# Two transformer blocks on one core: two fp16 parts for q and k, scores of two heads together, bias tiles and some weight splits on GpSimd

## The reference

```python
xn = layernorm(x)
x = x + attn0(xn) + experts(xn)        # block 0
xn = layernorm(x)
x = x + attn1(xn) + ternary_ffn(xn)    # block 1

# attn0, 16 heads of 16: bias from rel * slope and a causal mask
scores = q @ k.T * 16 ** -0.5 + rel * slope[h]; scores[causal] = -inf
attn = maximum(softmax(scores), 1e-10)
# experts: 8 of 256 -> 256 -> 256, all computed, weighted by token
out = sum_e w[e] * ((silu(xn @ Wg[e]) * (xn @ Wu[e])) @ Wd[e])
# attn1: the same without slopes and without the clamp
# ternary_ffn: W1 (1024x256) and W2 (256x1024) become alpha * sign(W) where |W| > delta
delta = 0.05 * max|W|; alpha = sum(|W| where |W| > delta) / count
y = gelu(xn @ W1q.T + b1) @ W2q.T + b2
# the result y of all 8 batches is rounded to 15 levels of one scale
scale = max|y| / 7 + 1e-8; y = clip(round(y / scale), -7, 7) * scale
```

## Time and profile before

| | |
|---|---|
| median of 3 runs | 858.34 us |
| the profiled execution | 856.29 us |
| its span on the core | 854.6 us |
| mean granted TensorE clock | 0.918 |
| PE, DVE, ACT, POOL busy | 684.0, 614.7, 588.4, 178.2 us |
| first pass | 0 to 142.4 us |
| six steady passes | 142.4 to about 697.5 us |
| last pass, final pass | to about 803 us, to 854.6 us |

### The profile page before, as it was taken

How to read it: one execution, slowest core, us unless ns; L and a number is a source line. 1 busy time by engine, 2 the same in 40 slices (tenths; PEclk the granted TensorE clock), 3 DMA queues, 4 the chain that set the end, 5 groups by cost and what they waited for, 6 DMA issues and landing times.

```text
span 854.6 us, 19350 instructions
## 1 busy us (share of the span) xinstructions
PE 684.0 (80%) x5856; PEld 539.7 (63%) x5856; DVE 614.7 (72%) x2239; ACT 588.4 (69%) x1753; POOL 178.2 (21%) x205
## 2 busy tenths in 40 slices
PE   0686544889878997989798997899798978897756
PEld 0464433668756785868676875688576856685533
DVE  3978746887677876787688767787678776766364
ACT  2455421887759794888488775979498848966764
POOL 6011021132113211131113211321113111320222
PEclk9889876999989998999989997999899999998975
DMA  6752005040413123130504040312313050300661
GB/s 194 267 148 87 1 1 160 2 148 16 128 48 111 37 79 108 40 109 13 174 1 148 13 145 30 111 37 87 100 57 91 13 160 2 124 26 1 191 202 52
DMA packets 55195, 73.94 MB, mean 87 GB/s; under 512 B 4544, under 2 KB 47680, under 8 KB 55104
## 3 DMA queue, kind: packets, MB, share of 16 engines
q1 hardware_dynamic: 52064, 69.22, 26.2%
q0 software_dynamic: 1056, 2.62, 1.0%
q10 hardware_dynamic: 1984, 1.21, 0.5%
HBM read 42.10 MB, written 30.93 MB: 85 GB/s over the span
## 4 chain that ended last, share of the span: by engine, by line
PE 39%; ACT 19%; DVE 18%; issue 15%; DMA 6%; ACTq 1%; SPq 1%; DVEq 1%; POOL 1%; POOLq 0%
PE gen_ps L972 9%; PE gen_ps L983 6%; ACT probs L875 5%; PE value_ps L1056 4%; PE gen_ps L1015 4%; DVE probs L1321 3%; PE gen_ps L946 3%; DVE probs L1332 3%; PE gen_ps L1003 3%; ACT hid L859 3%; ACT pt L884 3%; PE turn_ps L1033 2%; PE gen_ps L958 2%; PE turn_ps L1035 2%; PE turn_ps L1034 2%
## 5 line engine op out<-in xcount | busy, mean ns | idle before, releaser
L875 ACT ACTIVATE probs<-probs,nmax 128x256 f32<-128x256 f32 (+1 forms) x512 | 227.3, 447 | 57.1 <-DVE nmax L1321 55.8
L1321 DVE CUSTOM_DVE_ANT_0 probs<-score_ps,bias 128x256 f32<-128x256 f32 (+1 forms) x512 | 158.6, 352 | 62.8 <-PE score_ps L1027 60.1
L744 POOL TENSOR_TENSOR h_lo<-hid,h_hi 128x512 f16<-128x512 f32 x64 | 76.0, 1187 | 419.6 <-ACT h_hi L852 405.1
L884 ACT ACTIVATE pt<-turn_ps 128x384 f32<-128x384 f32 x256 | 121.4, 477 | 38.5 <-PE turn_ps L1035 38.5
L972 PE MATMUL gen_ps<-xe_hi,gu_hi 128*128 128x256 f16 x512 | 103.8, 287 | 5.2 <-DVE v_sb L1192 4.6
L972 PE MATMUL gen_ps<-xe_lo,gu_hi 128*128 128x256 f16 x512 | 103.7, 286 | 0.0
L972 PE MATMUL gen_ps<-xe_hi,gu_lo 128*128 128x256 f16 x512 | 103.5, 286 | 0.0
L875 ACT ACTIVATION_READ_ACCUMULATOR probs<-probs,nmax 128x1 f32 x512 | 97.4, 190 | 0.0
L1026 PE MATMUL score_ps<-k_stack,q_stack 96*128 96x256 bf16 x256 | 72.9, 287 | 28.8 <-DMA k_stack<-scr_k 15.2
L1033 PE MATMUL turn_ps<-ident,probs 128*128 128x128 f32 x256 | 76.7, 299 | 21.0 <-DVE probs L1332 15.7
L1332 DVE TENSOR_SCALAR probs<-probs,rsum 128x256 f32<-128x256 f32 (+1 forms) x256 | 87.5, 384 | 4.6
(11 more groups left out here) (169 smaller groups left out, 1530.0 us busy)
## 6 DMA issues: line engine op xcount, KB each, us to landing
q_stack<-scr_q SPq DMA_DIRECT2D x32, 384.0 KB, 3.9
k_stack<-scr_k SPq DMA_DIRECT2D x32, 384.0 KB, 5.1
scr_q<-parts SPq DMA_DIRECT2D x16, 384.0 KB, 2.7
scr_k<-parts SPq DMA_DIRECT2D x16, 384.0 KB, 3.3
scr_q<-parts SPq DMA_DIRECT2D x16, 256.0 KB, 3.6
scr_k<-parts SPq DMA_DIRECT2D x16, 256.0 KB, 3.6
x<-in_x SPq DMA_DIRECT2D x8, 256.0 KB, 3.0
scr_q<-parts SPq DMA_DIRECT2D x16, 128.0 KB, 2.9
```

Source lines behind the costliest of these rows:

```text
L744: pool.tensor_tensor(h0_lo[:, e], hid0[:, e], h0_hi[:, e], ALU.subtract).then_inc(s_h0l, 1)
L875: last = act.activation(probs[:, k, lo:hi], probs[:, k, lo:hi], ACT.Exp, scale=-1.0, bias=nmax[:, k, j:j + 1], accum_out=total)
L884: act.activation(pt[:, slot:slot + 3].rearrange("p t q -> p (t q)"), turn_ps[s % 2][:, 0:3 * P], ACT.Copy).then_inc(s_ev, 1)
L1321: last = dve.tensor_tensor_reduce(out=probs[:, k, lo:hi], in0=g[:, lo:hi], in1=bias[:, blo:S], scale=-1.0, scalar=BIG, op0=ALU.add, op1=AL ...
```

## The change

1. **Two fp16 parts.** q and k are cut into two fp16 parts, so 4 products x 16 features, 64 rows. `r0`, `r1`, `m0`, `m1` are gone. `l0`/`l1` subtract once, from `rest` and the first part. A batch stores with four DMAs in place of six; a group of eight heads is loaded with four DMAs of 64 rows and half the heads each.
2. **Paired heads.** Odd heads lie on partitions 64 to 127 of the same operands. PE issues the scores of both heads at the even one, four matmuls, into both score banks, when all maxima before them have been taken.
3. **Bias tiles** are made by GpSimd: a cast and 8 instructions on 128x1024.
4. **Weight splits** 3, 5, 7, 9, 11 and 13: the low part by GpSimd, for which ACT scales the raw tile in place as well (one more copy of 128x1024 each).
5. **Over partitions.** The five all-reduces are replaced: PE turns the column of 128 values (steps `tmx`, `tsm`, `qmax`, each takes a `gen_ps` bank), DVE reduces over the free axis.
6. **Ternary sums.** GpSimd multiplies weight and signs (128x2048), ACT sums that and the squares of the signs with its accumulator, two passes.
7. **Reciprocal** of 128x16 sums, then a copy to 128x256.
8. In the final pass `w2` and `qmax` lose their lag of 8 places on DVE (now 1 and 0). Steps of one name are kept in turn by `in_turn`; `gate` and the first `down` of a pass have one more wait each.

```diff
-SPLITS = 6
+SPLITS = 4
...
-    ln1a rt1 0 ln1b gate:0 1 up:0 tr1 2 3 rt2 gate:1 q1 k1 4 r1 down:0 5 6 v1 up:1 m1 7 gate:2 w1:0 w1:1 w1:2
+    ln1a rt1 0 ln1b gate:0 1 up:0 tr1 2 3 rt2 gate:1 q1 k1 4 down:0 5 6 v1 up:1 7 gate:2 w1:0 w1:1 w1:2
...
+POOL_SPLITS = (3, 5, 7, 9, 11, 13)
...
-                    wait(sp, s_lo, i - 1)
+                    sp.wait_ge(*lo_done(i - 2))
...
+                if name == "setup" and st.arg == 1:
+                    pool.tensor_copy(rel, rel_i).then_inc(s_pool, 1)
...
+                    for c in range(4):
+                        four, shape = slice(4 * c, 4 * c + 4), [P, 4, S]
+                        pool.tensor_tensor(bias0[:, four], rel.unsqueeze(1).broadcast_to(shape),
+                                           slope_sb[:, four].unsqueeze(2).broadcast_to(shape), ALU.mult).then_inc(s_bias, 1)
+                        pool.wait_ge(s_bias, 2 * c + 1)
+                        pool.tensor_tensor(bias0[:, four], bias0[:, four], bias1[:].unsqueeze(1).broadcast_to(shape), ALU.add)\
+                            .then_inc(s_bias, 1)
+                if name == "split" and st.arg in POOL_SPLITS:
...
+                    pool.tensor_tensor(lo, raw[st.arg % 2], hi, ALU.subtract).then_inc(s_lop, 1)
...
-                    pool.partition_all_reduce(t_amax[:, i:i + 1], t_max[:, i:i + 1], P, R_MAX).then_inc(s_tp, 1)
...
+                if name == "tern" and st.arg % TERN_STEPS == 4:
...
+                    act.activation(w, w, ACT.Copy, accum_out=t_sum[:, i, 0:1]).then_inc(s_ts, 1)
...
+                    act.activation(w, t, ACT.Square, accum_out=t_sum[:, i, 1:2]).then_inc(s_ts, 1)
...
+                if name == "tmx":
...
+                    pe.transpose(g[:, 0:P], t_max[:, st.arg:st.arg + 1].broadcast_to([P, P]), ident[:]).then_inc(full[st.bank], 1)
...
-                    wait(pe, s_mx, heads_before(st, -1))
+                    wait(pe, s_mx, heads_before(st))
...
+                    for hp in range(2):
+                        pe.matmul(score_ps[hp][:, 0:S], q[rows[hp], i, P:S], k[rows[hp], i, :], start=True, stop=True)
...
-                if name in ("r0", "r1"):
...
-                                   esum1[:, st.arg % H // 8].rearrange("p t h -> p (t h)").unsqueeze(2)
+                    dve.tensor_copy(rsum1[:].rearrange("p t h c -> p (t h) c"),
```

More of the change, by code:

```diff
@@ L150, in order_of @@
             out.append((name, int(arg or 0), int(word.startswith("+")) - int(name in BLOCK1)))
-    return with_heads(out, last)
+    steps = iter(in_turn([x for x in out if not isinstance(x, int)], lambda x: (x[0], x[2], x[1])))
+    return with_heads([x if isinstance(x, int) else next(steps) for x in out], last)
 SPLIT = [("qk", 0), ("gu", 0), ("wd", 0), ("gu", 1), ("gu", 2), ("wd", 2), ("gu", 3), ("gu", 4), ("wd", 4), ("gu", 5),
          ("gu", 6), ("wd", 6), ("gu", 7), ("qk", 1)]
+POOL_SPLITS = (3, 5, 7, 9, 11, 13)
 def uses(order):
@@ L210, in stages @@
         users = last_users(kind, it)
-    out, place, after_down = [], 0, {}
+    out = []
+    places = {step[0:2]: i for i, step in enumerate(x for x in ORDERS[kind] if x[0] in ("down", "op0"))}
     use = USES_BEFORE[kind]
@@ L220, in stages, with behind @@
         if st.name == "up":
-            st.place = after_down.get(st.arg - 2, 0)
+            st.place = places.get(("down", st.arg - 2), -1) + 1
         if st.name in ("down", "op0"):
-            st.place = place
-            place += 1
-            if st.name == "down":
-                after_down[st.arg] = place
+            st.place = places[st.name, st.arg]
         out.append(st)
-    late = [i + lag.get(f"{st.name}:{st.arg}", lag.get(st.name, 0)) for i, st in enumerate(out)]
-    return [out[i] for i in sorted(range(len(out)), key=lambda i: (late[i], i))]
+    def behind(st):
+        for key in (f"{kind}.{st.name}:{st.arg}", f"{kind}.{st.name}", f"{st.name}:{st.arg}", st.name):
+            if key in lag:
+                return lag[key]
+        return 0
+    late = [i + behind(st) for i, st in enumerate(out)]
+    return in_turn([out[i] for i in sorted(range(len(out)), key=lambda i: (late[i], i))],
+                   lambda st: (st.name, st.n.off, st.arg))
 def last_users(kind, it):
@@ L935, in do @@
                     last.then_inc(full[st.bank], 1)
+                if name == "tmx":
+                    pe.wait_ge(s_t, TERN * st.arg + 1)
+                    g = take(st)
+                    pe.transpose(g[:, 0:P], t_max[:, st.arg:st.arg + 1].broadcast_to([P, P]), ident[:]).then_inc(full[st.bank], 1)
+                if name == "tsm":
+                    pe.wait_ge(s_ts, 2 * st.arg + 2)
+                    g = take(st)
+                    for a in range(2):
+                        last = pe.transpose(g[:, P * a:P * a + P], t_sum[:, st.arg, a:a + 1].broadcast_to([P, P]), ident[:])
+                    last.then_inc(full[st.bank], 1)
+                if name == "qmax":
+                    pe.wait_ge(s_q, 1)
+                    g = take(st)
+                    pe.transpose(g[:, 0:P], yred[:, 0:1].broadcast_to([P, P]), ident[:]).then_inc(full[st.bank], 1)
                 if name in ("q0", "k0", "q1", "k1"):
@@ L1093, in do @@
                        .then_inc(s_set, 1)
[L1094 to L1102 removed]
+                if name == "split" and st.arg not in POOL_SPLITS:
                     i = st.arg
[L1104 removed]
+                    dve.wait_ge(s_hi, his_done(i))
                     hi, lo = split_parts(i)
@@ L1379, in by_channel @@
     def by_channel(w):
-        w = w.reshape(-1, H, C).transpose(0, 2, 1)
+        heads = [8 * u + 2 * i + hp for u in range(2) for hp in range(2) for i in range(4)]
+        w = w.reshape(-1, H, C)[:, heads].transpose(0, 2, 1)
         return w.reshape(-1, P, 2).transpose(0, 2, 1).reshape(-1, H * C)
```

223 lines of the change are left out of this document (120 added, 103 removed), and 2 rows, old and new, of the table LAG.

## The result

The changed kernel takes 875.19 us (median of 4 runs, 871.66 to 876.3) where the kernel before took 858.47. The ratio is 1.0184 with a 95% interval of 1.0151 to 1.0218: it is slower, by 1.5 to 2.2%, where -32 us were forecast. The profiled execution took 871.66 us, with a span of 869.9 against 854.6, so 15.3 us are to be found in the two traces.

A forecast was written before the change was run, and what follows sets the result against it. No engine is full; waits bound it, the first pass set by DVE and what it waits for, a steady pass by PE. 856.3 - 11 - 15.6 - 4 - 1.5 = 824.2, 826 us on the median's basis; range 803 to 850.

The forecast's parts named there:

- Front, +12: Start of first pass: first scores at about 61 us, 12 us later, behind GpSimd's bias instructions and split 5; bounds +1 to +18.
- I put 1 us for each of four, so -12.6: Rest of first pass: DVE's 16.6 us of waits for GpSimd's all-reduces become 1 us for each of four, -12.6.
- if it came early: Rest of first pass: PE would stand behind GpSimd's product and ACT's sums if early, but the order leaves room.
- Half of DVE's 15.3 us in the first pass: Rest of first pass: 15.3 us of splits, sum passes and `r0` leave DVE; half counted, -7.6.
- I take +1.0 there and nothing at the other 15 pairs: Steady pass: waiting for all earlier maxima costs PE +1.0 us at heads 14 and 15, nothing at the other pairs.
- rival C: Slower: score banks no longer alternate, PE waits for the second maximum at 128 pairs, +48 us, 874 us; chance 0.13.
- over 4 us a pass: Sign in the steady passes: PE's idle time released by a maximum under 2 us a pass; over 4 is rival C.
- I take -0.05: Steady pass: scores of a pair on different rows gain 0.05 us, over 16 pairs -0.8 us a pass.
- Steady gaps, -2.6: Steady pass: of 3.25 us in three PE gaps ending with the probabilities' copy or scaling, 2.6 go.
- the terms without the pair: Steady pass: -2.6 us from PE's gaps and -0.2 from freed DVE time behind the last head.
- Last and final pass, -5.5: Last pass -4 us from reciprocal, copies and subtraction on the chain; final pass -1.5 from one reciprocal.
- The bounds of the first pass: Whole first pass: -11 us, from -20 (all DVE work, front +6) to +2 (front +18, stalls alone gained).

The follow-up runs named there:

- e2: Changed kernel, but bias tiles and all low parts of the weight splits made by DVE as in the kernel before; 863.45 us.
- e11: Changed kernel with splits 3 and 5 made by DVE, bias tiles and the other splits staying on GpSimd; 868.16 us.
- e9: Changed kernel with the PE steps tmx and tsm for the ternary weights, and the DVE steps after them, moved 1 to 4 places later in the first pass; 869.53 us.
- e3: Changed kernel, but maxima and sums over partitions of the ternary weights are GpSimd all-reduces again, and the two sum passes DVE's; 881.78 us.
- e7: Kernel before, but PE issues both heads' scores at the even one, once all earlier maxima are taken; 96 rows, no row groups; 888.8 us.
- e4: Changed kernel with the edits of e1, e2 and e3 together; 870.8 us.
- e5: Kernel of e4, but score operands have 96 rows again, 64 of data and 32 of zeros, with one load each for q and k; 839.22 us.
- e1: Changed kernel, but each head's scores are issued at its own place and wait for all maxima but the last one; 876.51 us.
- e6: Changed kernel with the edits of e1, e2 and e5, keeping its maxima and sums by PE, GpSimd and ACT; 835.99 us.

## Why the prediction was wrong, step by step

- **Front, +12: right,** +11.5. The line through the two rows gave 2.35 us for 128x1024; the additions took 2.34 where alone, the products 1.89. That GpSimd's work does it is shown by e2; that the load for split 7 waits ahead of the stores, by e11, where the first scores come 6.7 us earlier without that wait. e11 also shows a second mechanism that was priced too low: DVE itself is held up, 8.8 us there, even in its smallest instructions. I had counted 0.87 us for each of three to five meetings, and on GpSimd's side.
- **"I put 1 us for each of four, so -12.6": failed.** DVE's 16.6 us went, but it waits 9.0 for the turns, and the turns that replace the all-reduces stand in PE's queue and hold up everything behind them, 23.4 us. PE also came back slower: it stood idle for 7.6 us up to 83.91 and for 7.1 up to 114.82, and behind each stall the granted clock is at 0.50, the lower of its two levels (1.2 of 2.4 GHz), for over 5 us of work:

```profile
83.90:89.50 5.60, 5.59 (x32) 2.96 (x33) 2.88 (x11) 3.25 (x7) 1.10 (x1) 0.50 0.02 5
...
114.80:120.00 5.20, 5.18 (x25) 3.77 (x26) 1.59 (x5) 1.44 (x5) 0.00 (x0) 0.50 0.00 0
```

  The prediction has no term for that; PE's busy time behind the first scores rose by 3.7 us. I had written that PE would stand behind the sums "if it came early" and took from the order, without following it in time, that it would not. e9 shows it was the place: moved back by a few steps they cost 7.5 us. By e3 this part is still worth 6.6 us, not 12.6.
- **Half of DVE's 15.3 us in the first pass: mostly lost.** DVE's busy time fell by 7.6 us and not by the 15.3 of the work that left, because the time in which it is held up counts as busy. Beside the GpSimd product of 2048 columns the scaling of one head at 100.46 took 3.83 us instead of 0.55. How much of the rest is held-up time was not added up, and the 7.6 us didn't shorten the part.

```profile
99.87 4.07 POOL L811 TENSOR_TENSOR hid<-hid,t_sb 128x2048 f32<-128x2048 f32 x1 [5.02 <-DVE t_sb L1185]
```

```profile
100.46 3.83 DVE L1392 TENSOR_SCALAR probs<-probs,rsum 128x256 f32<-128x256 f32 x2
...
104.95 0.55 DVE L1392 TENSOR_SCALAR probs<-probs,rsum 128x256 f32<-128x256 f32 x2
```

- **"I take +1.0 there and nothing at the other 15 pairs": failed.** It is +4.8 in a steady pass (5.1 against 0.3), in four waits, and 55.9 - 13.4 = 42.5 us over the program, 0.33 per pair, above the 0.25 from which rival C decides. By the prediction's own sign (over 4 us a pass) that is rival C. e7 shows that the early wait costs 30.5 us by itself. I had looked for the step that DVE was ahead by in the kernel before, where the second score of a pair comes later; issuing it earlier uses up just that lead.
- **"I take -0.05" for a pair: failed.** At the place shown above it is +0.08 (0.42 against 0.34). That the rows run side by side was right, and a price of 0.14 for leaving the mode was read from the earlier trace rows; but going in costs another 0.09 and going out 0.15, in all 0.24. On average over a pass the pair term is nearer 0, since PE is as busy as before, where -0.8 was forecast. In the changed kernel this price only takes away what side by side gains; with single heads, which visit twice as often, it costs 31.6 us (e4 to e5), and that is why taking out the pair alone (e1) did not help.
- **Steady gaps, -2.6: the right kind, too large.** The gaps before value products and turns fell by 25.5 us over the program, but in e5, without the early wait and without 64 rows, only by 5.9 (38.3 to 32.4). Where neither pairs nor rows disturb, in e5, a steady pass is 1.1 us shorter, where the terms without the pair were -2.8.
- **Last and final pass, -5.5: right in sum,** -6.3, though not in place. The last pass gained nothing; that the pair's price took it there too is likely and was not tested by itself. The end gained 6.5, of which 3.9 is one store of x; no run tells whether that belongs to the change.

The chain at that place before, and after with the copy that took the reciprocal's place:

```profile
802.92 6.08 DMA x_dram<-yx_sb
```

```profile
824.73 2.17 DMA x_dram<-yx_sb
...
844.95 0.68 DVE rsum L1400
```

The steps that failed are thus two waits: that for the pair's second bank, put at +1.0 a pass and at nothing for 15 of 16 pairs, which is +4.8; and the new turns, for which DVE was to wait 4 us and waits 9.0, with a wait of PE behind them that was put at nothing and is 23.4. With them goes the pair's gain of 0.8 us a pass, which is not there. The bounds of the first pass were also added wrongly: all DVE work counted and a front of +6 give -24.7 and not -20.

Rival C, at 874 us, named the wait, and the time too, but that is in part luck: its price was 48 us and e7 gives 30.5, and a good part of the distance lies in the first pass, which C takes over from the forecast. Nor is the wait the whole of it in a steady pass: e1 takes the waits away and stays at 876.5, because single heads visit the 64-row form twice as often. Only with both taken out (e5, e6) is the kernel faster than before, and e6 lands 1.2% above the forecast of 826. It is not the kernel of the forecast, though: its bias tiles and splits are on DVE, which is worth 11.7 us by e2. The changed kernel with nothing but single heads on 96 rows was not run.

The Trainium skill ("TensorEngine Tiling (Array Packing)", section "Key Properties") says that a change of mode drains TensorE. This case agrees and gives the price, 0.24 us for a visit between full matmuls. Its section "Theoretical Speedup" gives up to twice the speed for at most 64 rows; a pair's large matmuls reach it (0.12 us for two of 256 columns), and the pair does not, since a visit holds only 0.18 us of work.

The same skill ("SBUF — State Buffer", section "🔬 SBUF: two separate sides") says that an instruction of VectorE with two SBUF inputs and one of GpSimd that reads SBUF exclude each other for a whole instruction. The 2.30 us for an instruction on 16 columns with two inputs (e11) agrees: it ends with the GpSimd instruction beside it.
